# A V product of a batch issued behind the second FFN up product, in a gated cross-attention layer with a ternary FFN

## The chip, the cores and the metric

The kernel runs on one core of one Trainium2 chip. The metric is the device time of one launch in microseconds (us). Engines: PE is TensorE's matmul, DVE is VectorE, ACT is ScalarE, POOL is GpSimd, SP is the queue that issues the DMAs.

## The reference

Eight batches of 512 rows by 512 columns, 16 heads of 32, hidden width 2048:

```python
xn = layernorm(x)
Q, K, V = xn @ WqT + bq, ctx @ WkT + bk, ctx @ WvT + bv           # per head
qk = einsum("bhqd,bhkd->bhqk", Q, K); scores = qk / sqrt(dk)
feats = [scores.mean(), scores.max(-1).mean(-1), var(softmax(scores), ddof=1).mean(-1)]   # per head
t = exp(clip(mlp(feats), log 0.1, log 10))                         # gelu, gelu, linear
attn = softmax(qk / (2 * t))
x = x + tanh(g_xattn) * ((attn @ V) @ WoT + bo)
h = gelu(bitlinear(layernorm(x), w1)); x = x + tanh(g_ffn) * bitlinear(h, w2)
# bitlinear: rows quantised to 8 bits by their own maximum, weights to -1, 0, 1 times one scale
```

## The kernel before

The temperature of a head needs statistics over its whole score matrix, so each score tile is computed twice. A first pass (`score_a`, 64 tiles of 128x512 a batch) makes the row maximum on DVE (L916), an exponential on ACT (L734) and its statistics on DVE (L921). A second pass (`score_b`) makes the scores again, its exponential on ACT (L751), and on PE the sums with V and with ones.

The batches are pipelined. Iteration i works on three of them: the first pass of batch i, the second pass and FFN of batch i-1, and the projections K, V, Q of batch i+1. Iterations 1 to 6 have all three parts. They are a hardware loop of three turns with two bodies each. Iterations -1, 0, 7 and 8 are written out and lack parts. `stages(i)` gives `has_a`, `has_b`, `has_p` for the three.

The order is written out by hand, once for each engine, and each engine takes its own list strictly in that order. On PE a steady iteration runs: 16 sets of second-pass tiles mixed with first-pass tiles; then the K products; the W products (output projection of batch i-1); the transposes of the normalised x (L1380); the V products, one for each t of 0 to 3; two Q products; the transposes of the quantised rows (`xq`, L1430); two more Q products; the FFN up products `up(0)` and `up(1)` (L1439, fp8); and then for each of four row tiles the transposes `turn(t)` of the quantised hidden rows (L1450), `down(t-1)` (L1474) and `up(t+2)`.

K, W, V and Q are `split_product`s: operands split in a high and a low fp16 half, 12 matmuls of 512 columns (L1265), and for V and W a thirteenth that adds the bias (L1268). First-pass tiles lie between them (`tiles_a(point)`). In a steady iteration each W and V product has one in front of it and each K and Q product has two. At most four first-pass tiles are in flight: `score_a` of tile k waits for the exponential of tile k-4. ACT issues each exponential one tile late, DVE its statistics two tiles late.

Four PSUM banks (`b_ps` twice, `o_ps`, `z_ps`) are handed out in turn to every product, transpose and small matmul of the stage behind the sets. `bank_uses` lists them in PE's order, and `mm_use` turns a use into a bank and a count. PE fills a bank after `take` (the use four places earlier has been drained, `mm_free`), and the drainer waits on `mm_full`. V products are drained by ACT (L809) into `vbuf`, which only the next iteration's `values` reads; K and Q by ACT twice (L780, L784) with a remainder on POOL (L654); `xq` by DVE (t 0 and 2, L1060) and ACT (t 1 and 3); up products by ACT's gelu (L856); `turn(t)` half by ACT (`hidden_out`, L866), half by DVE (`turned_h`, L1093). Ahead of the Q products PE also waits with `drained` until all X and V banks are free.

In front of `turn(0)` DVE has a list of its own: the statistics of the last tiles, the head features, the row maxima of the first hidden tile (L1070), and its quantisation `quantise_h` (L1084), which releases `turn(0)`. V products read `c_hi` and `c_lo`, the halves of the context, which POOL writes for the next batch at the start of the next iteration (`split_c`, L583, L585).

Of the kernel before, what the change touches and what calls it, by code (L numbers as in the profile page):

```python
# [31 lines left out]
T = S // P  # L32
# [85 lines left out]
def bank_uses(setup, has_p, has_b, has_a):  # L118

    def some(stage, count, present=True):  # L120
        return [(stage, k) for k in range(count)] if present else []

    uses = some("S", 2, setup == 0) + some("K", C, has_p) + some("W", T, has_b)
    if setup == 0:
        uses += some("V", T, has_p) + some("X", T, has_p)
    else:
        uses += some("X", T, has_p) + some("V", T, has_p and setup is None)
    uses += some("Q", C, has_p)[:2] + some("xq", T, has_b) + some("Q", C, has_p)[2:]
    uses += some("V", T, has_p and setup == -1)
    uses += some("up0", NB, has_b) + some("up1", NB, has_b)  # L130
    for t in range(T):
        if has_b:
            uses += some(f"turn{t}", 2)
            if t > 0:
                uses += [(f"down{t - 1}", 0)]
            if t + 2 < T:
                uses += some(f"up{t + 2}", NB)
        if has_a and t < 3:
            uses += [("M", 0), ("M", 1)] if t == 0 else [("M", 1 + t)]
    uses += some(f"down{T - 1}", 1, has_b)  # L140
    return {use: n for n, use in enumerate(uses)}
# [66 lines left out]
def flamingo_kernel(nc, x, ctxT, g_xattn, g_ffn, WqT, bq, WkT, bk, WvT, bv, WoT, bo,  # L208
                    w1T, b1, w2T, b2, w3T, b3, f1T, f2T, out):
    with ExitStack() as ctx:  # L210
# [345 lines left out]
        def _(pool):  # L556
# [89 lines left out]
            def body(i, par):  # L646
# [59 lines left out]
                if second:  # L706
                    make_ternary(7)

            iterations(pool, pool_waits, body)


        @block.scalar
        def _(act):
# [40 lines left out]
            def body(i, par):  # L754
# [47 lines left out]

                def v_out():
                    for t in range(T):
                        tiles_a(C + T + t)
                        if has_p:
                            bank_n, before = mm_use(i, "V", t)
                            act_waits.wait_ge(mm_full[bank_n], before + 1)
                            nc.scalar.activation(vbuf[1 - par][:, t, :], mm_ps[bank_n][:, :], ACT.Copy,  # L809
                                                 scale=1.0 / WSCALE).then_inc(mm_free[bank_n], 1)  # L810
# [8 lines left out]
                else:  # L819
                    if second:  # L820
                        act_waits.wait_ge(tern_dve, 3)
                    v_out()
                if second:
# [45 lines left out]
                if has_b:  # L869
                    gelus(0)  # L870
                    gelus(1)
                for t in range(T):
                    if has_b:
# [365 lines left out]
        def _(pe):  # L1239
# [80 lines left out]
            def body(i, par):  # L1320
# [62 lines left out]

                def v_products():
                    for t in range(T):
                        rows = slice(t * P, (t + 1) * P)
# [6 lines left out]
                        if has_p:  # L1393
                            split_product(take(i, "V", t), [lambda c, x=x: x(c, rows) for x in c_parts],
                                          [lambda c, w=w: w["v"][:, c, :] for w in (w_hi, w_lo)], tiles_a(C + T + t),
                                          bias=0)
                        else:
# [6 lines left out]
                else:  # L1404
                    v_products()
                if second:
                    turned_x()
                if has_p:
                    for t in range(T):
                        drained(i, "X", t)  # L1410
                        if not first:
                            drained(i, "V", t)
# [64 lines left out]
                if has_b:  # L1477
# [4 lines left out]
                    up(0)  # L1482
                    up(1)
                for t in range(T):
                    if has_b:
                        turn(t)
                        if t == T - 1 and has_a:
                            early(0)
# [72 lines left out]
```

## Time and profile before

| | |
|---|---|
| time, median of 3 runs | 1399.98 us (1399.79 to 1400.82) |
| time of the profiled execution | 1399.59 us, its span 1397.5 us |
| mean granted TensorE clock | 0.945 |
| PE, DVE, ACT busy | 86%, 79%, 66% of the span |
| six steady iterations | `turn(0)` released at 322.05 us in the first, 1105.07 us in the sixth, by the start of L1084 |

The starts of L1084 lie 156.6 us apart on average ((1105.07 - 322.05) / 5). Rows of a timeline give a start, a duration and the instructions merged into the row. A matmul of 512 columns is shown as about 0.38 us long, since its pipeline drain is counted, while its successors start some 0.22 us apart: differences of starts are the measure for PE, not the sums of durations.

### The profile page before, as it was taken

Reading aid. Unit: us, or ns where it says so; the run is one execution under the profiler, and the core shown is the slowest. Engines: PE = TensorE matmul, PEld = TensorE weight load, DVE = VectorE, ACT = ScalarE, POOL = GpSimd, SP = SyncE. Lnnn points to the kernel's source line nnn. Section 1 sums busy time; section 2 is a strip of 40 time slices with the busy share of each in tenths; the row PEclk is TensorE's granted clock in tenths of the full one; section 3 lists DMA queues with packets and bytes.
Section 4 is the critical chain, followed back from the end, with each engine's and each line's share of the span. In section 5 each row is a group of like instructions: output and inputs, shape, how many; then the busy total and the mean of one; then the engine's idle time right before and its main releaser. Section 6 shows DMA issues by size and latency. Waiting matters only on the chain.

```text
span 1397.5 us, 23484 instructions
## 1 busy us (share of the span) xinstructions
PE 1200.2 (86%) x6684; PEld 444.2 (32%) x6684; DVE 1106.7 (79%) x2054; ACT 924.1 (66%) x1527; POOL 422.3 (30%) x399
## 2 busy tenths in 40 slices
PE   5635769998989899998999899998999899869958
PEld 2201321344224431344224431344224431233224
DVE  6298779887898869887898869887898879983246
ACT  5463679755985669665985669665985679645713
POOL 4279374510253114510253114510253101100210
PEclk9857879999999999999999999999999999979979
DMA  8710221112212221112112221102212210001000
GB/s 295 220 56 5 62 76 51 34 24 62 61 46 46 46 71 54 24 24 62 61 46 46 46 73 52 31 16 62 61 46 46 46 61 1 1 1 61 1 0 30
DMA packets 35475, 73.71 MB, mean 53 GB/s; under 512 B 7953, under 2 KB 7953, under 8 KB 34833
## 3 DMA queue, kind: packets, MB, share of 16 engines
q1 hardware_dynamic: 35344, 72.13, 17.9%
q8 instruction: 63, 1.03, 0.3%
q14 instruction: 68, 0.55, 0.1%
HBM read 38.39 MB, written 8.39 MB: 33 GB/s over the span
## 4 chain that ended last, share of the span: by engine, by line
PE 52%; DVE 26%; issue 9%; ACT 8%; POOL 1%; SPq 1%; DMA 1%; DVEq 1%; ACTq 0%; POOLq 0%
PE b_ps L1265 11%; DVE stat L921 7%; PE o_ps L1265 6%; PE o_ps L1474 5%; DVE nmax L916 5%; PE z_ps L1265 5%; PE o_ps L1305 4%; ACT region L751 4%; PE a_ps L1286 4%; PE b_ps L1292 4%; ACT etile L734 3%; PE b_ps L1439 2%; PE z_ps L1474 2%; PE b_ps L1450 2%; PE z_ps L1316 2%
## 5 line engine op out<-in xcount | busy, mean ns | idle before, releaser
L734 ACT ACTIVATE etile<-a_ps,nmax 128x512 f32<-128x512 f32 x512 | 369.5, 733 | 141.0 <-DVE nmax L916 140.8
L916 DVE TENSOR_REDUCE nmax<-a_ps 128x1 f32<-128x512 f32 x512 | 346.0, 677 | 54.0 <-PE a_ps L1286 50.2
L751 ACT ACTIVATE region<-b_ps,inv2t 128x512 f32<-128x512 f32 x512 | 354.8, 758 | 49.5 <-PE b_ps L1292 45.4
L921 DVE BATCH_NORM_STATS2 stat<-etile 128x6 f32<-128x512 f32 x512 | 347.6, 682 | 12.7 <-ACT etile L734 12.3
L1286 PE MATMUL a_ps<-kst,qst 96*128 96x512 f16 x512 | 202.4, 399 | 61.8 <-ACT etile L734 46.9
L1292 PE MATMUL b_ps<-qst,kst 97*128 97x512 f16 x512 | 192.6, 388 | 20.9 <-DVE region L1093 7.7
L1305 PE MATMUL o_ps<-region,vbuf 128*32 128x512 f32 x1024 | 138.0, 606 | 12.7 <-ACT region L751 7.1
L1316 PE MATMUL z_ps<-region,ones 128*32 128x512 f32 x1024 | 136.2, 604 | 8.4 <-DVE region L941 8.4
L654 POOL TENSOR_TENSOR region<-region 128x512 f16<-128x512 f32 x64 | 76.1, 1190 | 221.2 <-ACT region L784 221.0
L1292 PEld LDWEIGHTS b_ps<-qst,kst 97*128 97x128 f16 x512 | 49.1, 96 | 290.2 <-ACT region L751 258.9
L610 POOL TENSOR_TENSOR region<-region 128x512 f32<-128x512 f32 x32 | 40.9, 1278 | 291.4 <-DVE region L948 291.4
L1070 DVE TENSOR_REDUCE hmax<-region 128x1 f32<-128x512 f32 x128 | 82.2, 680 | 19.4 <-ACT region L856 18.3
L583 POOL CAST c_hi<-cin 128x512 f16<-128x512 f32 x28 | 17.1, 611 | 240.1 <-DMA cin<-in_ctxT_dram 239.5
L1286 PEld LDWEIGHTS a_ps<-kst,qst 96*128 96x128 f16 x512 | 50.7, 100 | 112.6 <-ACT etile L734 58.0
L1474 PE MATMUL o_ps<-f,region 128*128 128x512 fp8e4 x352 | 79.6, 379 | 0.0
L1439 PE MATMUL b_ps<-f,region 128*128 128x512 fp8e4 x256 | 65.3, 395 | 7.8 <-DVE region L1093 4.9
L866 ACT ACTIVATE region<-b_ps 128x1024 f16<-128x1024 f16 x31 | 31.7, 1024 | 49.3 <-PE b_ps L1450 48.6
L631 POOL TENSOR_SCALAR cin<-cin,mv,rstd 128x512 f32<-128x512 f32 x28 | 58.0, 2081 | 2.8 <-POOL rstd L622 2.6
L856 ACT ACTIVATE region<-b_ps,xmax 128x512 f32<-128x512 f32 x64 | 42.8, 691 | 19.9 <-PE b_ps L1439 19.7
L1450 PE MATMUL b_ps<-ident,region 128*128 128x128 f16 x488 | 35.4, 230 | 18.4 <-DVE region L1084 18.4
L938 DVE TENSOR_SCALAR region<-o_ps 128x512 f32<-128x512 f32 x32 | 21.7, 679 | 37.0 <-PE o_ps L1305 37.0
L620 POOL TENSOR_SCALAR rstd<-mv 128x2 f32<-128x2 f32 (+1 forms) x23 | 5.4, 233 | 143.3 <-DVE mv L1193 87.3
(278 smaller groups left out, 2001.4 us busy)
## 6 DMA issues: line engine op xcount, KB each, us to landing
kst<-region SPq DMA_DIRECT2D x96, 128.0 KB, 2.3
qst<-region SPq DMA_DIRECT2D x96, 128.0 KB, 2.3
xres<-in_x_dram SPq DMA_DIRECT2D x8, 1024.0 KB, 5.9
out_dram<-xres SPq DMA_DIRECT2D x32, 256.0 KB, 2.1
cin<-in_ctxT_dram SPq DMA_DIRECT2D x30, 256.0 KB, 2.7
cin<-in_x_dram SPq DMA_DIRECT2D x28, 256.0 KB, 2.6
kst<-in_f1T_dram SPq DMA_DIRECT2D x2, 1024.0 KB, 12.0
qst<-in_f2T_dram SPq DMA_DIRECT2D x2, 1024.0 KB, 10.7
```

What stands on the lines that cost most here:

```text
L734: nc.scalar.activation(etile[:, k % E_SLOTS, :], a_ps[k % A_BANKS][:, :], ACT.Exp, bias=nmax[:, slot_of(n), t:t + 1], scale=1.0).then_inc( ...
L751: nc.scalar.activation(probs[:, (s + 1) % 2, g, :], b_ps[g % 2][:, :], ACT.Exp, scale=inv2t[:, slot:slot + 1]).then_inc(b_exp, 1)
L916: vec.tensor_reduce(nmax[:, slot_of(k // T), k % T:k % T + 1], a_ps[k % A_BANKS][:, :], AX.X, ALU.max, negate=True).then_inc(a_max, 1)
L921: vec.bn_stats(stat[:, slot_of(k // T) * T + k % T, :], etile[:, k % E_SLOTS, :]).then_inc(a_stat, 1)
L1070: ins = vec.tensor_reduce(hmax[:, n:n + 1], hbuf[t % 2][:, n * S:(n + 1) * S], AX.X, ALU.max, apply_absolute_value=True)
L1265: ins = mat(mm_ps[bank_n][:, :], left[l](c), right[r](c), start=(c, l, r) == pairs[0], stop=bias is None and (c, l, r) == pairs[-1])
L1286: mat(a_ps[k % A_BANKS][:, :], qst[par][0:SHIFT, slot, t * P:(t + 1) * P], kst[par][0:SHIFT, slot, :], start=True, stop=True).then_inc(a_f ...
L1292: mat(b_ps[g % 2][:, :], kst[par][0:SHIFT + 1, slot, k * P:(k + 1) * P], qst[par][0:SHIFT + 1, slot, :], start=True, stop=True).then_inc(b ...
L1305: ins = mat(o_ps[g * DK:(g + 1) * DK, :], vbuf[par][:, k, n * DK:(n + 1) * DK], probs[:, (s + 1) % 2, g, :], start=k == 0, stop=k == T - 1)
L1316: ins = mat(z_ps[g * DK:(g + 1) * DK, :], ones32[:, 0:DK], probs[:, (s + 1) % 2, g, :], start=k == 0, stop=k == T - 1)
L1439: ins = mat(mm_ps[bank_n][:, :], xqT[:, c, t * P:(t + 1) * P], f1[:, c, n * S:(n + 1) * S], start=c == 0, stop=c == C - 1)
L1474: ins = mat(mm_ps[bank_n][:, :], hT[t % 2][:, k, :], f2[:, k, :], start=k == 0, stop=k == KC - 1)
```

## The change

In the iterations that have all three parts (1 to 6) the product V3 is taken out of the row V0, V1, V2, V3 and issued behind `up(1)`, in front of `turn(0)`. Its first-pass tile stays where it was and is issued alone. `bank_uses` moves the use in the same way, so every product from Q0 to `up(1)` gets the bank that its predecessor had. ACT drains V3 behind the gelus of `up(1)` and in front of `hidden_out(0)`. PE's waits in front of Q cover V0 to V2 only, and a wait for V3's drain stands behind `turn(1)`. POOL waits at the end of its iteration until V3 is complete. No instruction that computes is added or removed.

```diff
--- before.py
+++ after.py
@@ -124,10 +124,11 @@
     if setup == 0:
         uses += some("V", T, has_p) + some("X", T, has_p)
     else:
-        uses += some("X", T, has_p) + some("V", T, has_p and setup is None)
+        uses += some("X", T, has_p) + some("V", T - 1, has_p and setup is None)
     uses += some("Q", C, has_p)[:2] + some("xq", T, has_b) + some("Q", C, has_p)[2:]
     uses += some("V", T, has_p and setup == -1)
     uses += some("up0", NB, has_b) + some("up1", NB, has_b)
+    uses += some("V", T, has_p and setup is None)[T - 1:]
     for t in range(T):
         if has_b:
             uses += some(f"turn{t}", 2)
@@ -705,6 +706,9 @@
                         split_qk(n)
                 if second:
                     make_ternary(7)
+                if has_b and has_p:
+                    bank_n, before = mm_use(i, "V", T - 1)
+                    pool_waits.wait_ge(mm_full[bank_n], before + 1)
 
             iterations(pool, pool_waits, body)
 
@@ -800,9 +804,10 @@
                         nc.scalar.activation(xT[:, :, :, t * P:(t + 1) * P].rearrange("p l c n -> p (l c) n"),
                                              mm_16[bank_n], ACT.Copy).then_inc(mm_free[bank_n], 1)
 
-                def v_out():
-                    for t in range(T):
-                        tiles_a(C + T + t)
+                def v_out(rows=range(T)):
+                    for t in rows:
+                        if t < T - 1 or not (has_b and has_p):
+                            tiles_a(C + T + t)
                         if has_p:
                             bank_n, before = mm_use(i, "V", t)
                             act_waits.wait_ge(mm_full[bank_n], before + 1)
@@ -819,7 +824,9 @@
                 else:
                     if second:
                         act_waits.wait_ge(tern_dve, 3)
-                    v_out()
+                    v_out(range(T - 1) if has_b and has_p else range(T))
+                    if has_b and has_p:
+                        tiles_a(C + 2 * T - 1)
                 if second:
                     x_out()
                 for n in range(C):
@@ -869,6 +876,8 @@
                 if has_b:
                     gelus(0)
                     gelus(1)
+                    if has_p:
+                        v_out((T - 1,))
                 for t in range(T):
                     if has_b:
                         hidden_out(t)
@@ -1381,8 +1390,8 @@
                                                           x_split[t][:, l, c * P:(c + 1) * P], ident16[:, :])
                         ins.then_inc(mm_full[bank_n], 1)
 
-                def v_products():
-                    for t in range(T):
+                def v_products(tiles_of=range(T)):
+                    for t in tiles_of:
                         rows = slice(t * P, (t + 1) * P)
                         if first and t >= 2:
                             if t == 2:
@@ -1392,8 +1401,8 @@
                             score_a(0, 0, 2 * t - 3)
                         if has_p:
                             split_product(take(i, "V", t), [lambda c, x=x: x(c, rows) for x in c_parts],
-                                          [lambda c, w=w: w["v"][:, c, :] for w in (w_hi, w_lo)], tiles_a(C + T + t),
-                                          bias=0)
+                                          [lambda c, w=w: w["v"][:, c, :] for w in (w_hi, w_lo)],
+                                          tiles_a(C + T + t) if t < T - 1 or not has_b else (), bias=0)
                         else:
                             alone(tiles_a(C + T + t))
 
@@ -1402,13 +1411,15 @@
                 if first:
                     pe_waits.wait_ge(w_lo_done, 2)
                 else:
-                    v_products()
+                    v_products(range(T - 1) if has_b and has_p else range(T))
+                    if has_b and has_p:
+                        alone(tiles_a(C + 2 * T - 1))
                 if second:
                     turned_x()
                 if has_p:
                     for t in range(T):
                         drained(i, "X", t)
-                        if not first:
+                        if not first and (t < T - 1 or not has_b):
                             drained(i, "V", t)
                 for n in range(C):
                     cols = slice(n * P, (n + 1) * P)
@@ -1481,9 +1492,13 @@
                     pe_waits.wait_ge(tern_dve, 5)
                     up(0)
                     up(1)
+                    if has_p:
+                        v_products((T - 1,))
                 for t in range(T):
                     if has_b:
                         turn(t)
+                        if t == 1 and has_p:
+                            drained(i, "V", T - 1)
                         if t == T - 1 and has_a:
                             early(0)
                         if t > 0:
```

## Rows read from the trace of the kernel before

**Rows 1.** The page: busy us with share and count, and TensorE's granted clock.
```profile
PE 1200.2 (86%) x6684; PEld 444.2 (32%) x6684; DVE 1106.7 (79%) x2054; ACT 924.1 (66%) x1527; POOL 422.3 (30%) x399
...
PEclk9857879999999999999999999999999999979979
```

**Rows 2.** The chain that ended last, 590 to 672: start us, us, what.
```profile
608.78 2.59 PE z_ps L1265 x12
...
611.62 0.61 ACT vbuf L809
...
635.46 0.05 DVE region L1084
```

**Rows 3.** Timeline of PE, 605 to 640: start, us, instructions, idle before, releaser.
```profile
608.18 0.38 PE L1268 MATMUL o_ps<-bias,ones 128*128 128x512 f16 x1
...
608.62 0.38 PE L1265 MATMUL z_ps<-wv_hi,c_hi 128*128 128x512 f16 x1
...
611.21 0.38 PE L1268 MATMUL z_ps<-bias,ones 128*128 128x512 f16 x1
612.44 0.39 PE L1286 MATMUL a_ps<-kst,qst 96*128 96x512 f16 x1 [0.85 <-ACT vbuf L809]
...
620.20 0.40 PE L1430 MATMUL b_ps<-ident,region 128*128 128x128 f16 x4 [0.86 <-ACT region L784]
...
632.87 1.03 PE L1439 MATMUL z_ps<-f,region 128*128 128x512 fp8e4 x4
636.88 1.89 PE L1450 MATMUL b_ps<-ident,region 128*128 128x128 f16 x16 [2.99 <-DVE region L1084]
```

**Rows 4.** Timeline of DVE, same stage.
```profile
609.67 0.68 DVE L916 TENSOR_REDUCE nmax<-a_ps 128x1 f32<-128x512 f32 x1
...
610.88 0.67 DVE L916 TENSOR_REDUCE nmax<-a_ps 128x1 f32<-128x512 f32 x1
...
612.86 0.69 DVE L916 TENSOR_REDUCE nmax<-a_ps 128x1 f32<-128x512 f32 x1 [0.71 <-PE a_ps L1286]
...
618.93 0.42 DVE L1060 TENSOR_SCALAR region<-o_ps 128x512 f16<-128x512 f16 x1 [0.23 <-PE o_ps L1430]
...
625.40 0.69 DVE L916 TENSOR_REDUCE nmax<-a_ps 128x1 f32<-128x512 f32 x1 [0.22 <-PE a_ps L1286]
```

**Rows 5.** Timeline of ACT, same stage.
```profile
608.60 0.60 ACT L809 ACTIVATE vbuf<-o_ps 128x512 f32<-128x512 f32 x1 [1.85 <-PE o_ps L1268]
610.47 0.69 ACT L734 ACTIVATE etile<-a_ps,nmax 128x512 f32<-128x512 f32 x1 [1.28 <-DVE nmax L916]
...
618.78 0.69 ACT L780 ACTIVATE region<-b_ps,bqk 128x512 f32<-128x512 f32 x1 [0.52 <-PE b_ps L1265]
...
619.46 0.68 ACT L784 ACTIVATE region<-b_ps,bqk 128x512 f16<-128x512 f32 x1
...
633.93 0.69 ACT L856 ACTIVATE region<-z_ps,xmax 128x512 f32<-128x512 f32 x1 [0.18 <-PE z_ps L1439]
637.95 1.02 ACT L866 ACTIVATE region<-b_ps 128x1024 f16<-128x1024 f16 x1 [3.33 <-PE b_ps L1450]
```

**Rows 6.** Timeline of POOL after its last work of the iteration.
```profile
672.22 0.61 POOL L583 CAST c_hi<-cin 128x512 f16<-128x512 f32 x1 [42.72 <-DMA cin<-in_ctxT_dram]
```

**Rows 7.** Windows behind the gap: us, busy (count) per engine, granted clock, DMA.
```profile
634.00:642.00 8.00, 5.10 (x28) 2.96 (x28) 7.56 (x19) 3.02 (x4) 0.00 (x0) 0.79 0.48 109
642.00:669.00 27.00, 25.23 (x161) 12.81 (x161) 17.71 (x36) 13.31 (x21) 0.00 (x0) 1.00 0.09 32
```

**Rows 8.** Timeline of PE in the first steady iteration.
```profile
323.47 1.06 PE L1450 MATMUL b_ps<-ident,region 128*128 128x128 f16 x16 [2.99 <-DVE region L1084]
...
328.76 1.02 PE L1439 MATMUL b_ps<-f,region 128*128 128x512 fp8e4 x4 [1.63 <-DVE region L1093]
...
330.28 1.07 PE L1450 MATMUL b_ps<-ident,region 128*128 128x128 f16 x16
```

**Rows 9.** Timeline of PE in the third steady iteration, the same two transposes.
```profile
643.68 1.07 PE L1450 MATMUL b_ps<-ident,region 128*128 128x128 f16 x16
```

## The prediction

> **What bounds the kernel now.** I read the page first. PE is busy for 86% of the span and DVE for 79%, and the granted clock is at nine tenths or more in nearly every slice from the eighth on [rows 1]. No engine bounds the whole kernel, so the question is which one ends the waits where V3 is now and where it goes.
>
> For that I read the chain that ended last over one steady iteration, the third, and then each engine's timeline there. On the chain lie the matmuls of V3, ACT's drain of V3, and, further on, DVE's quantisation L1084 ahead of `turn(0)` [rows 2]. The timelines say how these hang together. PE issues the K, W and V products back to back. V3's first matmul starts at 608.62 and its last at 611.21. Q0's first-pass tile starts only at 612.44, having waited 0.85 us for ACT's drain of V3 [rows 3]. PE then runs through Q, `up(0)` and `up(1)`, whose last four matmuls start from 632.87. Then it is idle for 2.99 us until DVE has quantised, and `turn(0)` starts at 636.88 [rows 3]. The first steady iteration shows the same 2.99 us [rows 8].
>
> So before the gap the pace is PE's. At the gap it is DVE's, but DVE came there late because PE fed it the Q stage's score tiles late: DVE was waiting for PE when it took the last tile's maximum at 625.40 [rows 4]. The change takes work out of the PE-paced stretch and puts it into the idle one.
>
> **What is taken out in front of Q.** A matmul of 512 columns takes (611.21 - 608.62) / 12 = 0.216 us, start to start [rows 3]. V3 is 13 of them, 2.81 us. What Q waits for afterwards is the drain of V2. V2's last matmul starts at 608.18 and ACT takes it at 608.60 [rows 3, 5]. From ACT's start on V3 at 611.62 to PE's restart at 612.44 are 0.82 us [rows 2, 3], so PE restarts at 608.60 + 0.82 = 609.42. V3's first-pass tile keeps its place at about 608.40 and now runs inside this wait instead of ahead of a product. Q0 starts 612.44 - 609.42 = 3.02 us earlier. That is the most the step can be worth.
>
> **Whether the Q stage can run that much earlier.** First DVE. It is behind by two tiles at this point: V2's tile gets its maximum at 609.67, and V3's at 610.88 [rows 4]. That work does not move, since it stands behind DVE's layer norm and quantisation. A tile takes DVE 1.21 us (610.88 - 609.67). From V2's tile to the last tile of Q there are nine further tiles and two `xq` drains of 0.42 us, which I count at 0.45 with their issue. At full speed DVE could take the last maximum at 609.67 + 9 x 1.21 + 2 x 0.45 = 621.5. It takes it at 625.40 now, 3.9 us later, and 3.02 is asked of it. It has the room, and is caught up before the end.
>
> Second, the wait inside the stage. The fourth `xq` transpose starts at 620.20 after 0.86 us of waiting for ACT's drain of Q1 [rows 3]. ACT's second pass over Q1 starts at 619.46, 0.74 us ahead of PE's restart, and its first at 618.78, so the pair needs 0.68 us between them [rows 5]. After the change ACT must first do the exponential of Q1's first tile. Its maximum on DVE is the fourth after V2's tile, at 609.67 + 4 x 1.21 = 614.51. The step from a maximum to its exponential is 0.80 us (610.47 - 609.67, [rows 4, 5]), and an exponential takes about 0.6, so Q1's drain starts at 615.9, its second pass at 616.6, and PE restarts at 617.3: 2.9 us earlier than 620.20. The `xq` drain on DVE, which Q2's bank hangs on, starts at 618.93 now. It comes after the sixth tile from V2's, at 609.67 + 6 x 1.21 = 616.9, and ends at about 617.4, with PE asking for the bank at about 617.5. That is a tie, and some 0.2 us may be lost. I take 2.8 us for the stage, between 2.6 and 3.02. POOL's remainders and SP's twelve DMAs of Q hang on Q's drains and move with them. K's DMAs come before V.
>
> **What is put into the gap.** The last up product's four matmuls start from 632.87, so PE is free for the next at 632.87 + 4 x 0.216 = 633.73. The gap to `turn(0)` at 636.88 is 3.15 us, and V3 is 2.81 us [rows 3]. It fits with 0.34 us to spare. That holds as both ends of the gap move together: up products, gelus, features and L1084 all hang on the Q stage's end. V3's bank was `up1`'s first, long drained by ACT. If V3 started late or a matmul took longer, every 0.1 us beyond the 0.34 would delay `turn(0)` and with it DVE's next steps by 0.1. I cost the insertion at nothing; without the cover it would cost 2.81 us and the whole gain.
>
> The Trainium skill, page "TensorE: Matmul & The Clock Gate", section "Back-to-back issue gap", gives about 131 ns per matmul of 512 columns for a sustained stream of weight load and matmul. By it V3 would be 13 x 0.131 = 1.70 us and the gain 1.7 a batch; this case's trace disagrees, with 216 ns in such a stream, and the trace decides.
>
> **ACT, the waits, the other queues.** V3's drain of 0.6 us moves between the last gelu (633.93) and `hidden_out(0)` (637.95), where ACT is idle for 3.33 us [rows 5]. V3's last matmul would start at about 636.3, and ACT's drain 0.42 later, as for V2, at 636.7, done at 637.3. Only `hidden_out(0)` and the next gelus are queued behind it, and the former starts when the first transposes are complete, 637.5 at the earliest. So it costs nothing. No table load lies between the gelu at 633.93 and the copy at 637.95 [rows 5], so a copy between them needs none. `turn(0)` and `up(2)` now take banks one use later: the second half of `turn(0)` needs the third gelu of `up(1)`, `up(2)` the fourth (done near 634.6) and V3's drain. All are earlier than asked. The wait behind `turn(1)` comes some 6 us after that drain. POOL's new wait at its end stands in front of `split_c`, which starts at 672.22 after 42.72 us of idling [rows 6]; V3 is done 36 us earlier. SP waits for nothing new.
>
> **The granted clock.** In the third iteration it is 0.79 over the window with the gap and 1.00 after it: PE was idle, and part of the following work then ran at 1.2 instead of 2.4 GHz [rows 7]. `turn(0)` takes 1.89 us there, against 1.06 in the first iteration, which kept its clock [rows 3, 8]. Filling the gap should remove this. It is worth nothing: from `turn(0)` to `turn(1)` are 643.68 - 636.88 = 6.80 us in the third iteration and 330.28 - 323.47 = 6.81 in the first [rows 3, 8, 9], since DVE sets the pace between them.
>
> **The sum.** 2.8 us a batch, six batches: 16.8. The profiled execution took 1399.59 us, its span 1397.5 plus 2.1 around it, which does not change. 1399.59 - 16.8 = 1382.8. It lies 0.4 below the median of the runs, so I predict 1383.2 for the median. With 2.6 and 3.02 it is 1384.4 and 1381.9.
>
> **The rivals.**
> *V3 overruns the gap, or DVE does not catch up.* For it: the slack is only 0.34 us, and the Q stage has ties. Against it: the sums above. A loss of 0.8 to 1 us a batch leaves 1.8 to 2.0: 1388 to 1389.
> *Nothing is won: DVE is the true bound of the Q stage,* so `turn(0)` is not released earlier. For it: DVE has a backlog at V2's tile. Against it: its waits of 0.71 and 0.22 us for PE's tiles [rows 4], and 3.9 us of room. Time 1400.
> *Slower: the low clock moves to where PE sets the pace.* With the gap filled, PE's next idle stretch lies in front of the last matmuls of `up(2)` (1.63 us in the first iteration, [rows 8]). Were the clock to fall behind it, it would fall on the products up to `early`, where PE is on the chain. One visible spell costs 0.83 us on `turn(0)` alone and up to about twice that with the up matmuls behind it. The decision point is 2.8 us lost a batch, some 13 matmuls of 512 columns at half the clock (each 0.216 us longer). A loss of 4 us gives 1400 + 6 x 1.2 = 1407. Against it: in the first iteration this idle stretch was there and `turn(1)` still took 1.07 us [rows 8].
> *More: the clock regained is worth something.* 0.8 us a batch in five batches: 1379. Against it: 6.80 beside 6.81.
> *The matmuls removed are only worth 131 ns each,* because weight load and matmul overlap more than their starts show: 1.7 us a batch, 1389.8. The page named above speaks for it. Against it stand V3's thirteen evenly spaced starts.
>
> **How the numbers follow.** The forecast 80%; the overrun 8%; nothing won 3%; slower 4%; more 4%; the 131 ns case 1%. The range must leave out no more than 2 in 10. I let it reach from 1380.5 (a little of the clock comes back) to 1388.5 (an overrun of 0.8). It leaves out slower, nothing won, the 131 ns case and the far ends of two others, about 13%. A change of 0.2%, 2.8 us, is about what a measurement of this kernel can tell from none. Faster by more: 80 + 8 + 4 + 1 = 93%; within: 3%; slower: 4%.
>
> **What the changed profile would show.** PE's wait in front of Q0 for the drain of V2 some 0.8 us, with a lone score tile ahead of it; DVE with almost no waits from Q0 to the `xq` drains; the wait at the fourth `xq` transpose still there; the period of L1084 at 153.8 us instead of 156.6; V3's 13 matmuls between `up(1)` and `turn(0)` with 0.2 to 0.5 us idle behind them; 6.8 us from `turn(0)` to `turn(1)` as before, at the full clock. The prediction is wrong if `turn(0)` is released by PE and not by DVE, if DVE runs without waits to the end of Q, or if matmuls of 512 columns behind `turn(0)` start 0.43 us apart where PE paces.

## The result and the profile after

The changed kernel takes 1382.37 us (median of 4 runs, 1381.79 to 1383.72) against 1400.40 for the kernel before (4 runs): ratio 0.9875, 95% interval 0.9863 to 0.9887. The span of the profiled execution is 1380.5 us, where it was 1397.5. Forecast were 1383.2 us and 2.8 us a batch; measured is a gain of 18 us, and by the spans 17.0.

The page of the changed kernel has the same instruction counts on DVE and the same number of matmuls as [rows 1]:

```profile
PE 1193.1 (86%) x6684; PEld 440.3 (32%) x6684; DVE 1103.3 (80%) x2054; ACT 922.7 (67%) x1527; POOL 421.9 (31%) x399
...
PEclk9857879999999999999999999999999999979979
```

The third steady iteration on PE, to be read beside [rows 3] (start, duration, instructions, idle before, releaser). Lines have moved: L1277 is now the bias matmul, L1295 `score_a`, L1274 the product, L1441 the `xq` transposes, L1450 `up`, L1461 `turn`:

```profile
593.85 0.38 PE L1274 MATMUL b_ps<-wv_hi,c_hi 128*128 128x512 f16 x1
...
602.49 0.38 PE L1277 MATMUL o_ps<-bias,ones 128*128 128x512 f16 x1
602.71 0.38 PE L1295 MATMUL a_ps<-kst,qst 96*128 96x512 f16 x1
603.82 0.39 PE L1295 MATMUL a_ps<-kst,qst 96*128 96x512 f16 x1 [0.73 <-ACT vbuf L814]
...
611.57 0.40 PE L1441 MATMUL b_ps<-ident,region 128*128 128x128 f16 x4 [0.86 <-ACT region L788]
...
624.24 1.03 PE L1450 MATMUL o_ps<-f,region 128*128 128x512 fp8e4 x4
625.11 0.38 PE L1274 MATMUL z_ps<-wv_hi,c_hi 128*128 128x512 f16 x1
...
627.70 0.38 PE L1277 MATMUL z_ps<-bias,ones 128*128 128x512 f16 x1
628.26 1.06 PE L1461 MATMUL b_ps<-ident,region 128*128 128x128 f16 x16 [0.19 <-DVE region L1093]
...
633.55 0.81 PE L1450 MATMUL b_ps<-f,region 128*128 128x512 fp8e4 x3 [1.63 <-DVE region L1102]
```

V2's last matmul (602.49) is followed by the lone score tile (602.71), and Q0's first score tile, in short Q0's tile, starts at 603.82 after V2's drain. From V0's first matmul (593.85; 599.54 before) Q0's tile comes 9.97 us later, where it came 12.90 us later (612.44 - 599.54): 2.93 us less. The fourth `xq` transpose still waits 0.86 us and is 2.94 us earlier by the same measure. V3 stands at 625.11 to 627.70 and leaves PE idle for 0.19 us by the profile, which counts the pipeline's end. By starts, 627.70 + 0.22 to 628.26 are 0.34 us. `turn(0)` is 2.93 us earlier.

DVE in that stage, beside [rows 4] (L925 is the maximum, L1069 the `xq` drain):

```profile
603.98 0.68 DVE L925 TENSOR_REDUCE nmax<-a_ps 128x1 f32<-128x512 f32 x1
...
609.94 0.67 DVE L925 TENSOR_REDUCE nmax<-a_ps 128x1 f32<-128x512 f32 x1
...
611.13 0.41 DVE L1069 TENSOR_SCALAR region<-b_ps 128x512 f16<-128x512 f16 x1
...
612.23 0.69 DVE L925 TENSOR_REDUCE nmax<-a_ps 128x1 f32<-128x512 f32 x1 [0.36 <-PE a_ps L1295]
...
616.77 0.69 DVE L925 TENSOR_REDUCE nmax<-a_ps 128x1 f32<-128x512 f32 x1 [0.23 <-PE a_ps L1295]
```

In the kernel before DVE waited 0.71 us for the first tile of Q, 1.05 us for the first one behind the `xq` drains and 0.2 us for each of the others. Now it runs without a wait from 603.98 to 611.9, then waits 0.36, 0.23, 0.23 and 0.23 us. It is behind PE up to the `xq` drains and has some 1.05 us left behind them.

ACT, beside [rows 5] (L784 and L788 are the two passes of a Q drain, L814 a V drain, L863 a gelu, L873 `hidden_out`):

```profile
602.90 0.60 ACT L814 ACTIVATE vbuf<-o_ps 128x512 f32<-128x512 f32 x1 [1.85 <-PE o_ps L1277]
...
608.97 1.27 ACT L738 ACTIVATE etile<-a_ps,nmax 128x512 f32<-128x512 f32 x2
610.16 0.69 ACT L784 ACTIVATE region<-b_ps,bqk 128x512 f32<-128x512 f32 x1
...
610.84 0.68 ACT L788 ACTIVATE region<-b_ps,bqk 128x512 f16<-128x512 f32 x1
...
625.31 0.69 ACT L863 ACTIVATE region<-o_ps,xmax 128x512 f32<-128x512 f32 x1 [0.18 <-PE o_ps L1450]
628.11 0.60 ACT L814 ACTIVATE vbuf<-z_ps 128x512 f32<-128x512 f32 x1 [2.12 <-PE z_ps L1277]
628.92 1.02 ACT L873 ACTIVATE region<-b_ps 128x1024 f16<-128x1024 f16 x1 [0.21 <-PE b_ps L1461]
```

V3's drain (628.11) lies between the last gelu and `hidden_out(0)`, with no table load. The drain of Q1 (610.16) follows two exponentials without a break. Those wait for DVE's maxima, which matters further down.

The granted clock, beside [rows 7], is at full in the window of `turn(0)` too:

```profile
625.00:636.00 11.00, 9.18 (x71) 4.96 (x69) 10.41 (x23) 5.78 (x11) 0.00 (x0) 1.00 0.38 87
636.00:660.00 24.00, 22.39 (x133) 10.95 (x134) 14.87 (x32) 10.95 (x17) 0.00 (x0) 1.00 0.09 35
```

**A finer measure.** What lies ahead of the first steady iteration differs from one program or execution to the next: its first V0 matmul starts between 284.6 and 288.2 us in the fourteen profiled executions, and at 286.24 and 287.19 in two of the changed kernel. So for what follows I also give the distance from the first to the sixth table load ahead of the gelus of `up(0)` (L856 before), over five: the mean period of a steady iteration, from one profiled execution each. In the kernel before they lie at 314.74 and 1097.77, so 156.61 us; in the changed kernel at 311.93 and 1080.64, so 153.74. That is 2.87 us a batch.

The second and the fourth of the five distances hold the start of a turn of the hardware loop, where PE stands still for 0.6 to 2.1 us (last section). The first, third and fifth do not, and within a run they agree to 0.2 us or less unless the clock falls. The table gives them as "undisturbed". A fall of the clock where PE paces costs 1.1 to 1.7 us in the runs below, 0.2 to 0.35 in the mean period, and is named where it occurs.

### The profile page after: what moved, and what is told of

It is laid out like the page before. It is cut to its first block, busy times and chain, and to the rows that moved or that the text cites. A ratio compares the mean times of both kernels' runs of the same rounds, so it can differ in the third digit from the quotient of the medians.

```text
span 1380.5 us, 23490 instructions
## 1 busy us (share of the span) xinstructions
PE 1193.1 (86%) x6684; PEld 440.3 (32%) x6684; DVE 1103.3 (80%) x2054; ACT 922.7 (67%) x1527; POOL 421.9 (31%) x399
## 3 DMA queue, kind: packets, MB, share of 16 engines
q8 instruction: 62, 1.02, 0.3%
## 4 chain that ended last, share of the span: by engine, by line
PE 50%; DVE 27%; issue 10%; ACT 8%; POOL 1%; SPq 1%; DMA 1%; DVEq 1%; ACTq 0%; POOLq 0%
PE b_ps L1274 11%; DVE stat L930 7%; PE o_ps L1485 6%; DVE nmax L925 5%; PE o_ps L1274 5%; PE o_ps L1314 4%; PE z_ps L1274 4%; ACT region L755 4%; PE a_ps L1295 4%; PE b_ps L1301 4%; ACT etile L738 3%; DVE hmax L1079 2%; PE z_ps L1485 2%; PE b_ps L1450 2%; PE z_ps L1325 2%
## 5 line engine op out<-in xcount | busy, mean ns | idle before, releaser
L925 DVE TENSOR_REDUCE nmax<-a_ps 128x1 f32<-128x512 f32 x512 | 345.7, 677 | 41.7 <-PE a_ps L1295 37.9
L1295 PE MATMUL a_ps<-kst,qst 96*128 96x512 f16 x512 | 202.8, 401 | 60.8 <-ACT etile L738 49.8
L1079 DVE TENSOR_REDUCE hmax<-region 128x1 f32<-128x512 f32 x128 | 82.2, 680 | 19.5 <-ACT region L863 18.2
L1295 PEld LDWEIGHTS a_ps<-kst,qst 96*128 96x128 f16 x512 | 50.7, 100 | 111.9 <-ACT etile L738 57.9
L1450 PE MATMUL b_ps<-f,region 128*128 128x512 fp8e4 x256 | 65.3, 394 | 14.8 <-DVE region L1102 12.8
L863 ACT ACTIVATE region<-b_ps,xmax 128x512 f32<-128x512 f32 x64 | 43.4, 689 | 28.1 <-PE b_ps L1450 27.7
L873 ACT ACTIVATE region<-b_ps 128x1024 f16<-128x1024 f16 x31 | 31.7, 1023 | 32.0 <-PE b_ps L1461 31.2
L1274 PE MATMUL b_ps<-wo_hi,region 128*128 128x512 f16 x128 | 43.4, 399 | 5.7 <-POOL region L616 5.7
```

The lines of the kernel that those rows point to most:

```text
L925: vec.tensor_reduce(nmax[:, slot_of(k // T), k % T:k % T + 1], a_ps[k % A_BANKS][:, :], AX.X, ALU.max, negate=True).then_inc(a_max, 1)
L1079: ins = vec.tensor_reduce(hmax[:, n:n + 1], hbuf[t % 2][:, n * S:(n + 1) * S], AX.X, ALU.max, apply_absolute_value=True)
L1274: ins = mat(mm_ps[bank_n][:, :], left[l](c), right[r](c), start=(c, l, r) == pairs[0], stop=bias is None and (c, l, r) == pairs[-1])
L1295: mat(a_ps[k % A_BANKS][:, :], qst[par][0:SHIFT, slot, t * P:(t + 1) * P], kst[par][0:SHIFT, slot, :], start=True, stop=True).then_inc(a_f ...
L1450: ins = mat(mm_ps[bank_n][:, :], xqT[:, c, t * P:(t + 1) * P], f1[:, c, n * S:(n + 1) * S], start=c == 0, stop=c == C - 1)
```

## The experiments

All are measured against the kernel before on the same chip, whose median was 1400.0 to 1400.6 us in the three groups of runs. The ratio is not the quotient of the two medians and differs from it by up to 0.0014. The medians of different groups come from different chips.

| run | median us | ratio (95%) | mean period us | undisturbed distances us |
|---|---|---|---|---|
| before | 1400.4 | | 156.61 | 156.02 to 156.10 |
| changed | 1382.4 | 0.9875 (0.9863 to 0.9887) | 153.74 | 153.02 to 153.19 |
| changed, again | 1381.6 | 0.9858 (0.9843 to 0.9873) | 153.72 | 153.09 to 153.21 |
| V3 short in its old place | 1403.5 | 1.0008 (0.9994 to 1.0022) | 157.07 | 156.89 to 157.07, clock falls in all three |
| the same, waiting for V2 only | 1381.3 | 0.9858 (0.9830 to 0.9886) | 153.68 | 152.96 to 153.03 |
| before, waiting for V2 only | 1395.0 | 0.9961 (0.9949 to 0.9974) | 156.21 | 155.01 to 155.08 |
| changed, V3 short in the gap | 1380.2 | 0.9859 (0.9824 to 0.9894) | 153.66 | 152.96 to 153.03 |
| changed, V3 with 4 more | 1381.3 | 0.9856 (0.9827 to 0.9885) | 153.70 | 153.09 to 153.16 |
| changed, V3 twice as long | 1385.6 | 0.9903 (0.9887 to 0.9920) | 154.37 | 153.63 to 153.70 |
| changed, no V waits | 1378.6 | 0.9852 (0.9836 to 0.9869) | 153.69 | 152.98 to 153.06 |
| changed, V2 short | 1385.3 | 0.9902 (0.9885 to 0.9919) | 153.36 | 152.87 to 152.94 |
| changed, `xq` in pairs | 1376.2 | 0.9822 (0.9808 to 0.9835) | 152.59 | 151.97 to 152.04 |
| pairs and no V waits | 1376.5 | 0.9822 (0.9809 to 0.9835) | 152.85 | 151.61; 153.27 and 153.33 with a clock fall |
| before, `xq` in pairs | 1393.0 | 0.9951 (0.9937 to 0.9964) | 156.17 | 154.99 and 155.06; 156.06 with a clock fall |

### What the matmuls are worth, and what the wait is worth

Two runs shorten V3 in its old place. `only` cuts the list of pairs; the second edit is in the second run alone:

```diff
-                                          bias=0)
+                                          bias=0, only=1 if t == 3 and has_b else None)
```

```diff
-                        if not first:
+                        if not first and (t < T - 1 or not has_b):
                             drained(i, "V", t)
```

> The kernel before, with V3 in its old place cut from 13 matmuls to 2 (its first pair and the bias; the rest of the product is left out in the six steady iterations). If what counts is only the matmul time in front of Q, 11 x 0.216 = 2.4 us a batch go: 14 us less than before, near 1386. If ACT's order counts as well, less: V3's drain stands on ACT behind the exponential of V2's tile, which waits for DVE until 610.47, so the drain can't start before 611.1 and Q0 not before 611.9 (612.44 now). That is 0.55 us a batch, 3.3 in all, near 1397. I hold the second to be likelier.

> As the run with V3 cut in its old place (part of the product left out), and PE no longer waits for V3's drain ahead of Q0, but for V2's, as in the changed kernel. Both views expect Q0 about 2.6 to 3.0 us earlier a batch: 16 to 18 us less than before, 1382 to 1384. If this comes out as the run without this edit, the wait has no part in the gain.

With the matmuls alone gone the time is no shorter: 1403.5 us, ratio 1.0008 with an interval that holds 1. With the wait on V3's drain gone too it is 1381.3, the changed kernel's time. The third batch of the first run shows why, ACT first (L734 an exponential, L809 a V drain) and then PE (L1288 is `score_a`):

```profile
611.80 0.60 ACT L809 ACTIVATE vbuf<-o_ps 128x512 f32<-128x512 f32 x1 [1.85 <-PE o_ps L1270]
613.68 0.69 ACT L734 ACTIVATE etile<-a_ps,nmax 128x512 f32<-128x512 f32 x1 [1.28 <-DVE nmax L916]
614.26 0.59 ACT L809 ACTIVATE vbuf<-z_ps 128x512 f32<-128x512 f32 x1
```

```profile
612.04 0.38 PE L1270 MATMUL z_ps<-bias,ones 128*128 128x512 f16 x1
615.07 0.39 PE L1288 MATMUL a_ps<-kst,qst 96*128 96x512 f16 x1 [2.66 <-ACT vbuf L809]
```

V3's last matmul starts at 612.04, but its drain stands on ACT behind the exponential of V2's tile, which comes at 613.68 because DVE is still quantising. PE waits 2.66 us. From V0's score tile (602.51) Q0's comes 12.56 us later instead of 13.13 (612.44 - 599.31), so 0.57 us are won, as the second view has it. Even these do not show in the time, and that neither view had. The clock over the start of Q in the second, third and fourth iterations (windows; the clock is the figure before the last two):

```profile
455.90:459.40 3.50, 3.45 (x9) 1.31 (x10) 1.63 (x4) 1.22 (x2) 0.00 (x0) 0.54 0.00 0
615.00:618.50 3.50, 3.43 (x16) 1.57 (x17) 2.94 (x5) 1.35 (x3) 0.00 (x0) 1.00 0.00 0
770.40:774.00 3.60, 3.60 (x10) 1.35 (x11) 1.66 (x4) 1.15 (x2) 0.00 (x0) 0.55 0.00 0
```

In the second iteration the first six matmuls of Q0 start within 2.56 us (chain of work) instead of 1.30, at a granted clock of 0.54, close to the lower level of 1.2 GHz. The stage from Q0's first matmul to `up(0)` takes 15.51, 15.23 and 15.28 us in iterations 2, 4 and 6, and 13.83 in 1, 3 and 5, as in every iteration of the kernel before. So an idle stretch of 2.66 us, which all six iterations have ahead of work that PE paces, cost 1.4 to 1.7 us in three of them: 4.5 us, where six times 0.57, or 3.4 us, were won.

The wait alone, V3 whole and in its old place:

> The kernel before, whole, with one wait less: ahead of Q0 PE waits for V0 to V2 drained and no longer for V3 (the banks are still guarded by their own waits). V3 stays in its place. Q0 then starts right behind V3's last matmul, at 611.4 instead of 612.4: 1.0 us a batch, and DVE has 3.9 us of room: 6 us less, 1394. If DVE or the fourth xq transpose paces already, nothing: 1400.

```diff
-                        if not first:
+                        if not first and (t < T - 1 or not has_b):
                             drained(i, "V", t)
```

1395.0 us, 5 less, ratio 0.9961. In the second batch Q0's tile (454.08) now follows V3's last matmul (453.86) at once, and the three undisturbed distances between table loads are 1.0 us shorter (155.0 to 155.1 against 156.0 to 156.1). The other two, 158.90 and 157.03, were 157.31 and 157.57; the longer one holds a standstill of 2.08 us at the start of the turn and a granted clock of 0.76 over the 7 us behind it. So the 17 to 18 us are made up of the wait and the matmuls together: about 1.0 us a batch from the first (a wait on V2's drain, which is over sooner, takes 0.7 to 0.9 us, but a score tile runs in it), and the other 1.9 from the 13 matmuls. While Q0 waits for V3's drain, the matmuls taken out are worth 0.57 us at most.

### What V3 costs in the gap

```diff
-                                          tiles_a(C + T + t) if t < T - 1 or not has_b else (), bias=0)
+                                          tiles_a(C + T + t) if t < T - 1 or not has_b else (), bias=0,
+                                          only=1 if t == 3 and has_b else None)
```

and `only=16` and `only=25` in the other two.

> The changed kernel with V3 in the gap cut to 2 matmuls (the rest of the product left out). If V3 is fully hidden in the gap, its removal changes nothing: 1382.4, with 2.6 us of idling ahead of turn(0) and the granted clock falling there again as before. If V3 in the gap costs something, it is faster; if the clock that the filled gap keeps is worth something, it is slower by 0.8 us a batch or more, 1387.

> The changed kernel with four matmuls more in V3 (17 instead of 13; they add some pairs twice, so V3 is another product). They take 0.86 us, the idle time behind V3 is 0.35, so turn(0) starts 0.5 us later. By the prediction's words every 0.1 us beyond the gap delays DVE's next steps by 0.1: 3 us more, 1385.4. The other view: DVE needs turn(0) complete only for its next quantisation, 1.8 us after it is, and PE idles 1.63 us in front of the last matmuls of up(2): no change, 1382.4.

> The changed kernel with V3 about twice as long: 26 matmuls instead of 13 (the pairs twice and the bias; another product). That is 2.8 us more in the gap, of which 0.35 was free, so turn(0) starts 2.45 us later. If what is late at turn(0) is late everywhere: 14.7 us more, 1397. If there is room behind turn(0) (four matmuls more cost nothing, DVE needs turn(0) complete some 1.8 us after it is, PE idles 1.63 us ahead of the last matmuls of up(2)), only what is beyond it: 0.6 to 0.8 us a batch, 4 to 5 in all, near 1387.

V3 short in the gap: 1380.2 us (1378.8 to 1385.8), period 153.66 against 153.74. The total can't tell it from the changed kernel, the periods differ by 0.08 us, and the undisturbed distances by about 0.1. So V3 in the gap costs 0.1 us a batch at most. Behind the emptied gap the clock falls again in two of the six iterations, the third and the fifth, and that costs nothing either. PE there in the third iteration (L1464 is `turn`), then the window behind the gap:

```profile
624.27 0.38 PE L1279 MATMUL z_ps<-bias,ones 128*128 128x512 f16 x1
627.22 1.07 PE L1464 MATMUL b_ps<-ident,region 128*128 128x128 f16 x16 [2.57 <-DVE region L1093]
...
634.03 1.07 PE L1464 MATMUL b_ps<-ident,region 128*128 128x128 f16 x16
```

```profile
627.00:633.00 6.00, 5.78 (x31) 2.66 (x32) 5.74 (x14) 2.80 (x4) 0.00 (x0) 0.72 0.24 55
```

From `turn(0)` to `turn(1)` are 6.81 us at a clock of 0.72 over most of it, and 6.81 in the changed kernel (635.07 - 628.26) at full clock. The run with V3 short in its old place and no wait for it keeps the whole gap of 2.99 to 3.00 us, its clock falls behind it in all six iterations, and its period is 153.68 all the same.

Four matmuls more: 1381.3 us, period 153.70, nothing, though `up(2)` starts 4.56 us behind V3's first matmul, where it was 4.05. Twice as long: 1385.6 us, period 0.63 us longer. `up(2)` then starts 6.51 us behind V3's first matmul, 2.46 later, and DVE's timeline shows where the rest of it went (L1093 `quantise_h`):

```profile
628.37 1.29 DVE L1093 TENSOR_SCALAR region<-region,hsc 128x2048 f32<-128x2048 f32 x1
629.57 2.46 DVE L1079 TENSOR_REDUCE hmax<-region 128x1 f32<-128x512 f32 x4
...
633.33 1.28 DVE L1093 TENSOR_SCALAR region<-region,hsc 128x2048 f32<-128x2048 f32 x1 [0.41 <-PE b_ps L1464]
```

`turn(0)` starts at 632.23 there. DVE works on from 629.57 with the maxima of the second row tile and meets `turn(0)` only at its next quantisation at 633.33, for which it waits 0.41 us. The two quantisations lie 4.96 us apart instead of 4.68 (631.52 - 626.84), and the next one follows after 5.87 instead of 5.51 us, as two of its row maxima wait 0.18 us each for the gelus of `up(2)`. Together that is 0.64 us; the other 1.8 of the 2.46 us are absorbed.

### What holds the Q stage now

```diff
-                        if not first and (t < T - 1 or not has_b):
+                        if not first and not has_b:
                             drained(i, "V", t)
```

> The changed kernel without any wait for a V drain ahead of Q0 (banks still guarded). If PE still paces the Q stage, Q0 starts 0.9 us earlier a batch: 5 us less, 1377. If the stage is now held by the chain DVE maximum, exponential, drain of Q1, fourth xq transpose, PE just waits 0.9 us longer there: 1382, no change. I hold the second to be likelier, as ACT works without a break from 607.2 to 611.4 in front of that transpose in the changed kernel's third batch.

> The changed kernel with V2, too, cut to 2 matmuls in its place (the rest of that product left out). It asks whether a second product taken out of the stretch would pay again. If PE paced, 2.4 us a batch, 14 in all: 1368. If the backlog of DVE holds the stage (its quantisation ends at 604.0 whatever PE does, and the first maximum behind it is V2's), nothing or at most the 1.0 us a batch for which DVE still waits: 1376 to 1382; I expect 1382.

Without any V wait the median is 1378.6 us, the period 153.69: no change by the period. The spans of the profiled executions differ by 3.7 us (1376.8 against 1380.5). Of these 1.6 lie ahead of the first steady iteration (its first V0 matmul starts at 284.69, not 286.24) and 1.9 behind the sixth table load, in the iterations that are written out, where the clock differs: 0.68 over 27 us from 1205 in the changed kernel, 0.75 over 27 us from 1203 here. Neither place holds a wait that this edit takes out. PE in the third batch (L1441 the `xq` transposes) gains 0.9 us at the start of Q and gives it back whole at the fourth transpose, where it waits 1.74 us instead of 0.86:

```profile
608.16 0.39 PE L1441 MATMUL z_ps<-ident,region 128*128 128x128 f16 x4
610.29 0.40 PE L1441 MATMUL b_ps<-ident,region 128*128 128x128 f16 x4 [1.74 <-ACT region L788]
```

With V2 short PE waits 2.00 us there, and the period is 153.36, 0.38 less. Of this about 0.2 come from shorter standstills at the start of the turns (0.56 and 0.66 us, where the changed kernel has 0.94 and 1.43); by the undisturbed distances about 0.2 us a batch are won for 2.4 us of matmuls taken out. The time does not show even that: the median is 1385.3, the four runs lie between 1380.3 and 1387.5 us, the profiled one at 1380.3. Falls of the clock behind the longer wait, as with V3 short in its old place, would explain the slower ones, but the profiled execution has none in its steady iterations, and the mean clocks (0.949 in it, 0.948 to 0.950 in the others) don't decide it. That stays open.

So in the changed kernel PE no longer sets the pace from Q0 to the fourth `xq` transpose. That transpose takes the bank of Q1, which ACT drains behind two exponentials, which wait for DVE's backlog. The edit that follows from it lets no transpose need the product just ahead of it: two behind Q0, two behind Q1, the bank uses and drains alike.

```diff
-    uses += some("Q", C, has_p)[:2] + some("xq", T, has_b) + some("Q", C, has_p)[2:]
+    q, turned = some("Q", C, has_p), some("xq", T, has_b)
+    uses += q[:1] + turned[:2] + q[1:2] + turned[2:] + q[2:]
...
-                    if has_b and n == 1:
-                        for t in range(T):
+                    if has_b and n < 2:
+                        for t in (2 * n, 2 * n + 1):
```

> The changed kernel with the four xq transposes split: two behind Q0, two behind Q1, their uses of the banks and their drains on ACT and DVE split in the same way. No transpose then needs the drain of the product just in front of it, so PE's wait of 0.86 us ahead of the fourth goes. DVE waits about 1.0 us a batch between that transpose and the end of Q, so it can follow: 0.8 us a batch, 5 in all, near 1377.5. If DVE holds the stage, nothing: 1382.

> The run with the xq transposes in pairs, and no wait for V drains ahead of Q0. PE gets 0.9 us more at the start of Q. DVE had some 1.0 us of waits in the changed kernel from the fourth transpose to the end of Q, of which the pairs use 0.8, so at most 0.2 us a batch remain: as the run with the pairs alone within 1.5 us, near 1376.5. If PE paces still: 5 us less than it.

> The kernel before with the xq transposes in pairs, V3 in its old place. PE paces here and DVE has 3.9 us of room, so the whole 0.86 us a batch is won: 5 us less, 1395. If the pairs only work together with the moved V3, 1400.

> The changed kernel once more beside the three others of this call, as their measure: 1382 to 1383, by every view.

The pairs take the changed kernel from 1381.6 to 1376.2 us beside each other (five and four runs, 1373.8 to 1377.1 against 1379.9 to 1383.3), the period from 153.72 to 152.59. It is the fastest version of this study: ratio 0.9822 to the kernel before. The transposes on PE and the end of Q on DVE (L1442 the transposes, L926 the maximum):

```profile
602.80 0.61 PE L1442 MATMUL b_ps<-ident,region 128*128 128x128 f16 x8
...
606.28 0.39 PE L1442 MATMUL z_ps<-ident,region 128*128 128x128 f16 x4
606.50 0.39 PE L1442 MATMUL b_ps<-ident,region 128*128 128x128 f16 x4
...
612.79 1.03 PE L1451 MATMUL z_ps<-f,region 128*128 128x512 fp8e4 x4
```

```profile
599.93 0.69 DVE L926 TENSOR_REDUCE nmax<-a_ps 128x1 f32<-128x512 f32 x1
...
611.69 0.69 DVE L926 TENSOR_REDUCE nmax<-a_ps 128x1 f32<-128x512 f32 x1 [0.22 <-PE a_ps L1296]
```

PE runs from Q0's tile to `up(0)` without waiting, in 12.80 us instead of 13.83. That is 1.03 us, where 0.8 were expected: the wait of 0.86 us at the fourth transpose, in which the profile leaves out the pipeline's end, is 1.02 by starts (611.57 - 610.33 - 0.22 in the changed kernel). DVE works from 599.93 without a wait until the last tile, for which it waits 0.22 us: its slack is nearly spent.

Taking the V waits away as well gives 1376.5 us, nothing more, as expected; but two things lie under this that the expectation did not have. The one undisturbed distance is 0.4 us shorter (151.61 against 152.0). And in the first and fifth iterations the clock falls behind the idle stretch of 1.63 us in front of the last matmuls of `up(2)`, which is the place that the prediction's rival "slower" named. PE in the first iteration, where it falls, then in the second, where it doesn't (L1451 is `up`, L1486 `down`), and the windows of both:

```profile
325.65 1.02 PE L1451 MATMUL b_ps<-f,region 128*128 128x512 fp8e4 x4 [1.63 <-DVE region L1103]
...
328.77 4.58 PE L1486 MATMUL o_ps<-f,region 128*128 128x512 fp8e4 x16
...
481.40 3.62 PE L1486 MATMUL o_ps<-f,region 128*128 128x512 fp8e4 x16
```

```profile
325.65:334.65 9.00, 9.00 (x50) 4.92 (x51) 5.70 (x12) 2.43 (x5) 0.00 (x0) 0.81 0.02 4
478.98:487.98 9.00, 9.00 (x58) 4.77 (x59) 6.87 (x14) 3.73 (x7) 0.00 (x0) 1.00 0.09 33
```

From this idle stretch to the `up` behind `down(0)` are 7.53 us in the first iteration (333.18 - 325.65) and 5.88 in the second (484.86 - 478.98), and the first and fifth distances are 1.7 us longer than the third. These two falls cost 3.3 us, more than six times 0.4.

The pairs in the kernel before give 1393.0 us, 7.6 us less (6.9 by the ratio), where 5 were expected. Its mean period is only 0.44 shorter, but it comes from the slowest of the five runs (1397.7 us) and holds two spells of the low clock that the kernel before does not have: one more behind the gap of the third iteration (0.57 over 634 to 642; from that table load to the next one are 31.22 us instead of 30.13), and one behind a standstill of 1.52 us at the start of the third turn (0.76 over 825 to 832). The distances without them, 154.99 and 155.06, are 1.0 us shorter than before, and the stage itself, Q0's first matmul to `up(0)`, is 1.03 us shorter (12.80 against 13.83).

## Why the prediction was right

**The stage that paces.** Right, with a part left unsaid. Q0 3.02 us earlier was forecast and 2.93 measured (PE restarts 0.92 us behind the start of V2's drain, not 0.82). The prediction followed the drain of V2 and got the number, but it listed the gain under what is taken out in front of Q, as if the 2.81 us of matmuls were it. The runs show that they are worth 0.57 us a batch at most, and nothing in the time, while Q0 waits for V3's drain. That drain is held on ACT behind an exponential that waits for DVE's maximum.

**DVE's room.** Right: 3.9 us of room, 2.9 used, 1.05 left in the trace. The pairs left 0.22 of that.

**The wait inside the stage.** Right: the fourth transpose forecast 2.9 us earlier and measured 2.94. The tie at Q2's bank lost nothing: the tile of Q2 follows at 611.81. So 2.87 a batch came out instead of 2.8 (2.9 by the undisturbed distances).

**The gap.** 0.34 us to spare forecast, 0.34 measured. Wrong was the sentence that every 0.1 us beyond it would delay DVE's next steps by 0.1, and that V3 without its cover would cost 2.81 us and the whole gain. Four matmuls more cost nothing, and thirteen more cost 0.63 us a batch (0.5 by the undisturbed distances), not 2.4. `turn(0)` has some 1.8 us of slack of its own. I took the release at the gap for a link of the chain that ends last. The chain there runs along DVE and not through PE. The kernel before had it so already, in the line that follows the last of [rows 2] but for DVE's issue time (L1070 the next row maxima), and the prediction did not read on:

```profile
636.66 2.47 DVE hmax L1070 x4
```

In the changed kernel it is the same (L1093 is `quantise_h`, L1079 the row maxima):

```profile
626.84 0.05 DVE region L1093
...
628.04 2.47 DVE hmax L1079 x4
```

**ACT, the waits, the queues, the clock.** Right: drain in the idle stretch, no table load, POOL and SP moved with the rest, and the regained clock worth nothing (6.81 us from `turn(0)` to `turn(1)` with and without it; five falls in the six gaps of the kernel before, none in the steady iterations of the changed one).

**The rivals.** The overrun did not happen and would have cost less. Nothing won: refuted. More from the clock: refuted by V3 short in the gap, and by the run with the whole gap and a fall in every iteration (153.68). The 131 ns case: refuted by the time and by V3's twelve steps of 0.216 us in the gap. The rival on the other side, the low clock where PE paces, did not come in the twelve steady iterations of the changed kernel that were profiled, but it is real. It took the gain of V3 short in its old place, and with pairs and no V waits it came at the very place that the prediction named, at 1.65 us an iteration. The argument against it, one iteration with this idle stretch and a full clock, was thin: of 48 such stretches of 1.63 to 1.64 us in all profiled executions the clock fell behind two. That the changed kernel was spared is partly luck.

## What to carry to other kernels

Taking a product out of a stage pays its matmul time only if no wait behind it ends as late as before. Look at what is queued on the draining engine in front of the drain, and shorten the wait together with the work. After such a move ask again which engine sets the pace. Here the drain of Q1, held up on ACT by DVE's backlog, had become the next hold, and splitting the transposes into pairs won 1.1 us a batch more.

Before you call a release in front of an idle stretch critical, read the chain on past it and see when the released work is next needed. And a gap that the clock falls behind costs nothing where another engine sets the pace behind it, but 1.1 to 1.7 us here where PE does, which can be more than the edit that opened the gap has won.

## What the runs showed of the hardware that was not expected

The granted clock falls behind some idle stretches of PE and not behind others of the same length in the same place. In the steady iterations of the fourteen profiled executions it fell behind 22 of the 30 gaps of 2.98 to 3.00 us in front of `turn(0)` (in the kernel before five of six, not in the first iteration [rows 8]), behind three of the six stretches of 2.66 us, two of the six of 2.57, none of the six of 2.00 or of the six of 1.74, and two of the 48 of 1.63. It also fell behind a standstill of 2.08 and one of 1.52 us. What decides it is not shown.

The iterations that begin a turn of the hardware loop (the third and fifth) are longer: 157.31 and 157.57 against 156.0 to 156.1 us for the others before, 154.41 and 154.90 against 153.0 to 153.2 after. At their start PE stands still in the middle of the first `values` for 0.6 to 2.1 us with nothing that the profile shows as a releaser. First the changed kernel, then the kernel before waiting for V2 only:

```profile
507.35 0.59 PE L1314 MATMUL o_ps<-region,vbuf 128*32 128x512 f32 x1 [0.94 <-issue]
```

```profile
513.25 0.59 PE L1305 MATMUL o_ps<-region,vbuf 128*32 128x512 f32 x1 [2.08 <-issue]
```

Its length differs from one program to the next by more than a microsecond. It goes into the mean periods, so that differences of 0.2 to 0.3 us between them can come from it alone. What PE waits for there was not tried.
